# Two attention layers with routed experts: GpSimd's indirect DMAs moved to the end of a step, routing one step shorter, stores moved to SyncE

## The reference

```python
x = x + tanh(g_xattn[0]) * L0_xattn(layernorm(x), ctx, ctx)   # 16 heads of 8, softmax
x = x + tanh(g_ffn[0])   * L0_ffn(layernorm(x))               # 8 experts, top 2 per token, gelu
x = x + tanh(g_xattn[1]) * L1_xattn(ctx, ctx, layernorm(x))   # 16 heads of 8, masked softmax
x = x + tanh(g_ffn[1])   * L1_ffn(layernorm(x))               # 4 experts, all computed, weights gated
```

## Time and profile before

| | |
|---|---|
| three timed runs | 1296.69, 1297.87, 1298.11 us; median 1297.87 |
| the profiled execution's own time | 1297.54 us |
| its span, first to last instruction | 1295.9 us |
| busy share of the span | PE 89%, PEld 74%, DVE 72%, ACT 55%, POOL 47% |
| chain that ended last | PE 74%, issue 8%, POOL 5%, ACT 4%, DVE 4%, SPq 3%, DMA 1% |
| layer 0 attention, 20 to 335 us | PE busy 296.5 of 315.0, granted clock 0.97 |
| its tail and the plan, 335 to 419 us | PE busy 42.0 of 84.0, granted clock 0.68 |
| expert stage, 419 to 683 us | PE busy 258.4 of 264.0, POOL 153.3 |
| start of layer 1, 683 to 713 us | PE busy 5.7 of 30.0 |
| layer 1 attention, 713 to 1066 us | PE busy 328.3 of 353.0, granted clock 0.98 |
| dense experts, 1066 to 1296 us | PE busy 209.1 of 230.0 |

### The profile page before, as it was taken

The page is one execution under the profiler, slowest core; times in us unless marked ns, Lnnn a source line. Parts: engine busy times, 40 slices in busy tenths (PEclk is TensorE's granted clock), DMA queues, the critical chain, the costliest instruction groups (busy, mean ns, idle before and its releaser), DMA issues.

```text
span 1295.9 us, 41850 instructions
## 1 busy us (share of the span) xinstructions
PE 1147.0 (89%) x13375; PEld 965.1 (74%) x13375; DVE 933.0 (72%) x3267; ACT 718.8 (55%) x1554; POOL 613.2 (47%) x828
## 2 busy tenths in 40 slices
PE   4799999899861999999992899999899985999998
PEld 3577777677650999999991677777677765999997
DVE  4578888688756544444442799999898858888887
ACT  3588877688640555555550566666566642444443
POOL 2123555465675555665556555555555323121220
PEclk9899999899875999999995899999999997999999
DMA  6501111111112222222213222222222100000000
GB/s 187 183 27 35 53 58 52 44 51 53 49 40 79 74 73 73 73 73 73 69 58 108 67 68 67 66 66 65 60 71 61 50 2 1 25 17 24 16 24 25
DMA packets 85622, 76.42 MB, mean 59 GB/s; under 512 B 35160, under 2 KB 66648, under 8 KB 85464
## 3 DMA queue, kind: packets, MB, share of 16 engines
q1 hardware_dynamic: 73816, 48.14, 13.2%
q0 software_dynamic: 11648, 26.24, 6.5%
HBM read 50.21 MB, written 23.07 MB: 57 GB/s over the span
## 4 chain that ended last, share of the span: by engine, by line
PE 74%; issue 8%; POOL 5%; ACT 4%; DVE 4%; SPq 3%; DMA 1%; POOLq 1%; DVEq 0%; ACTq 0%
PE ps_m L1429 10%; PE ps_p L1636 9%; PE ps_m L1584 8%; PE ps_p L1417 8%; PE ps_s L1389 5%; PE ps_s L1379 5%; PE ps_s L1451 3%; PE ps_s L1570 3%; PE ps_s L1469 3%; PE ps_s L1624 2%; PE ps_s L1626 2%; PE ps_s L1572 2%; PE ps_s L1571 2%; PE ps_s L1625 2%; PE ps_m L1405 2%
## 5 line engine op out<-in xcount | busy, mean ns | idle before, releaser
L926 DVE TENSOR_REDUCE mx<-ps_s 128x8 f32<-128x512 f32 x256 | 169.9, 685 | 57.0 <-PE ps_s L1379 56.9
L1429 PEld LDWEIGHTS ps_m<-Vbd,PT 128*64 128x64 f32 x4096 | 140.2, 138 | 57.6 <-issue 52.3
L687 ACT ACTIVATE PT<-ps_p 128x512 f32<-128x512 f32 x256 | 153.0, 598 | 30.3 <-PE ps_p L1417 27.8
L1417 PE MATMUL ps_p<-cst,Pr 128*128 128x128 f32 x1024 | 161.8, 283 | 8.6 <-ACT PT L687 4.8
L1429 PE MATMUL ps_m<-Vbd,PT 128*64 128x18 f32 x4096 | 163.7, 213 | 0.1
L533 POOL TENSOR_TENSOR spare<-spare 1x1 f32<-1x1 f32 x148 | 29.2, 197 | 263.9 <-PE ps_s L1626 142.3
L844 ACT ACTIVATE Kbd<-ps_s,c 128x512 f32<-128x512 f32 x128 | 87.6, 687 | 118.1 <-PE ps_s L1626 117.6
L588 POOL DMA_INDIRECT w1a<-louts,gi x128 | 124.6, 973 | 41.1 <-issue 36.2
L1584 PE MATMUL ps_m<-xn3T 128*128 128x128 f32 x1152 | 140.0, 275 | 0.2 <-ACT xn3T L810 0.2
L1417 PEld LDWEIGHTS ps_p<-cst,Pr 128*128 128x128 f32 x1024 | 119.9, 145 | 22.8 <-issue 15.9
L1584 PEld LDWEIGHTS ps_m<-xn3T 128*128 128x128 f32 x1152 | 134.7, 192 | 0.4 <-issue 0.4
(11 more groups left out here) (209 smaller groups left out, 2659.7 us busy)
## 6 DMA issues: line engine op xcount, KB each, us to landing
ctxg<-in_ctxT SPq DMA_DIRECT2D x64, 256.0 KB, 2.7
xn3T<-lists SPq DMA_DIRECT2D x72, 128.0 KB, 2.1
louts<-xn3T POOLq DMA_DIRECT2D x72, 128.0 KB, 2.4
Kbd<-in_ctxT SPq DMA_DIRECT2D x512, 8.0 KB
out<-x SPq DMA_DIRECT2D x16, 256.0 KB, 2.3
w1a<-in_L_ffn_W SPq DMA_DIRECT2D x1, 2048.0 KB, 9.7
w1a<-louts,gi POOLq DMA_INDIRECT x128
lists<-xn3T,pos POOLq DMA_INDIRECT x96, 2.2
```

What stands on the lines that cost most here:

```text
L687: return nc.scalar.activation(dst, src, ACT.Copy)
L926: V.tensor_reduce(mx[g.par][:, q, :], per_key(ps_s[:, q, :]), AX, ALU.max).then_inc(max_done, 1)
L1417: ins = turn(ps_p[:, c % 2, P * i:P * i + P], Pr[g.par][:, j // 2, col:col + P], ident)
L1429: ins = mm((bank7, bank6)[pr][S * b:S * b + S, VW * j:VW * (j + 1)], PT[c][:, P * i + S * b:P * i + S * b + S], Vbd[g.par][:, 2 * pr + b, ...
```

## The change

- GpSimd's order in a step becomes: constant rows of g-1, inverse deviations, then the indirect DMAs. The wait for the scores is gone. In layer 0 the scattered group is g-8 rather than g-9.
- `both_choices` joins `second_choice` inside step e+4, `ranks` moves to the end of step e+4, `route_places` to the start of step e+5.
- Tail blocks are routed in steps 28, 30, 32 and 34 rather than 29, 31, 33 and 34; the scatters of the last steps are dealt out in slots, six indirect DMAs in each of the steps 28 to 32, ten in step 33, none in 34, eight in 35.
- The stores of the expert stage go from GpSimd to SyncE, where they stand between the loads: load of tile k+6, store of tile k.

```diff
--- before.py
+++ after.py
@@ -84,8 +84,9 @@
 
 MAIN = GROUPS - STEPS
 RB = 4
-TAIL = {25: 29, 27: 31, 29: 33, 31: 34}
-LAST_ROWS = {29: (20,), 30: (21, 22), 31: (23, 24), 32: (25, 26), 33: (27,), 34: (28, 29), 35: (30, 31)}
+TAIL = {25: 28, 27: 30, 29: 32, 31: 34}
+LAST_ROWS = {28: ((20, 0, 1), (21, 0)), 29: ((21, 1), (22, 0, 1)), 30: ((23, 0, 1), (24, 0)), 31: ((24, 1), (25, 0, 1)),
+             32: ((26, 0, 1), (27, 0)), 33: ((27, 1), (28, 0, 1), (29, 0, 1)), 34: (), 35: ((30, 0, 1), (31, 0, 1))}
 BLOCKS = MAIN // RB + len(TAIL)
 
 
@@ -501,11 +502,22 @@
                 sp.dma_start(xin[k % 4], lists[bass.ds(r, ET), :].rearrange("(t p) d -> p t d", p=P)).then_inc(
                     rows_in[k % 4], 16)
 
-            for k in range(4):
+            def store_rows(u, k):
+
+                sp.wait_ge(yo_ready, at(u, k, 1, 1, 4))
+                sp.dma_start(louts[sl(at(u, k, ET, 0, 4), ET), :].rearrange("(t p) d -> p t d", p=P),
+                             yo[k % 2]).then_inc(rows_out[k % 2], 16)
+
+            for k in range(8):
                 load_rows(0, k)
-            with sp.Fori(1, NT // 4) as u:
+                if k >= 6:
+                    store_rows(0, k - 6)
+            with sp.Fori(2, NT // 4) as u:
                 for k in range(4):
                     load_rows(u, k)
+                    store_rows(u, k - 6)
+            for k in range(NT - 6, NT):
+                store_rows(0, k)
             sp.wait_ge(yo_ready, NT)
 
             for dst, src in ((v1.rearrange("p (e f) -> p e f", e=E1), A["L1_ffn_ew1"].rearrange("e d f -> d e f")),
@@ -556,12 +568,12 @@
                                         orow[g.layer][:, :].unsqueeze(1).to_broadcast([P, 2, DM]),
                                         ALU.add).then_inc(xc_ready, 1)
 
-            def scatter(g):
+            def scatter(g, slots):
 
                 pool.wait_ge(pos_ready, g.block(1))
                 pool.wait_ge(xn2_ready, g.count(2, 2))
                 carry(lambda: touch(g.par), g.at())
-                for slot in range(2):
+                for slot in slots:
                     for t in range(2):
                         if g.in_main():
                             i = 2 * (g.k % RB) + t
@@ -589,42 +601,28 @@
                                                      bass.IndirectOffsetOnAxis(ap=gi[i][:, c:c + 1], axis=0)
                                                      ).then_inc(gathered[i], 16)
 
-            def apart_from_scores(g):
-
-                if g.real():
-                    pool.wait_ge(s_done, g.count(4, 4))
-
             def step(g):
                 def have(d):
                     return g.plus(d).real()
 
-                if g.layer == 0:
-                    if isinstance(g.u, int) and g.k in LAST_ROWS:
-                        for k in LAST_ROWS[g.k]:
-                            scatter(Group(0, k, 0))
-                    elif have(-9):
-                        apart_from_scores(g)
-                        scatter(g.plus(-9))
-                if g.layer == 1 and have(4):
-                    apart_from_scores(g)
-                    gather(g.plus(4))
-                if g.layer == 1 and have(-1):
+                if have(-1):
                     rows_plus_constant(g.plus(-1))
                 if have(-2) or have(2):
                     inverse_deviations(g)
-                if g.layer == 0 and have(-1):
-                    rows_plus_constant(g.plus(-1))
+                if g.layer == 0:
+                    if isinstance(g.u, int) and g.k in LAST_ROWS:
+                        for k, *slots in LAST_ROWS[g.k]:
+                            scatter(Group(0, k, 0), slots)
+                    elif have(-8):
+                        scatter(g.plus(-8), (0, 1))
+                elif have(4):
+                    gather(g.plus(4))
 
             nc.gpsimd.memset(mask_in, 0.0).then_inc(mask_clear, 1)
             pool.wait_ge(setup_in, SETUP)
             pool.wait_ge(x_in0, 16)
             pool.wait_ge(orow_done, 1)
             steps(pool, 0, step)
-
-            def store_rows(u, k):
-                pool.wait_ge(yo_ready, at(u, k, 1, 1, 4))
-                pool.dma_start(louts[sl(at(u, k, ET, 0, 4), ET), :].rearrange("(t p) d -> p t d", p=P),
-                               yo[k % 2]).then_inc(rows_out[k % 2], 16)
 
             def low_weights(u, k):
 
@@ -641,11 +639,8 @@
             with pool.Fori(0, NT // 4 - 1) as u:
                 for k in range(4):
                     low_weights(u, k + 2)
-                    store_rows(u, k)
-            for k in range(NT - 4, NT):
-                if k + 2 < NT:
-                    low_weights(0, k + 2)
-                store_rows(0, k)
+            for k in range(NT - 4, NT - 2):
+                low_weights(0, k + 2)
             pool.wait_ge(rows_out[0], 16 * (NT // 2))
             pool.wait_ge(rows_out[1], 16 * (NT // 2))
             pool.wait_ge(place_ready, 1)
@@ -1086,12 +1081,9 @@
                 if g.layer == 0:
                     if isinstance(g.u, int) and g.k == 3:
                         layer1_constants()
-                    block = router_due(g, -6, 1)
+                    block = router_due(g, -5, 1)
                     if block:
                         route_places(block)
-                    block = router_due(g, -5, None)
-                    if block:
-                        both_choices(block)
                     now(statistics_in, 2)
                     now(maximum, 0, 2)
                     now(maximum, 0, 3)
@@ -1109,6 +1101,7 @@
                     block = router_due(g, -4, None)
                     if block:
                         second_choice(block)
+                        both_choices(block)
                     now(heads, -1, 0)
                     now(denominators, -1, 1)
                     now(heads, -1, 1)
@@ -1359,7 +1352,7 @@
                 if g.plus(-4).real():
                     pe.wait_ge(lg_read, g.plus(-4).count(1, 1))
                 pe.wait_ge(kq_ready, g.count(1, 1))
-                ranks_before = router_due(g, -6, 1) if g.layer == 0 else None
+                ranks_before = router_due(g, -5, 1) if g.layer == 0 else None
                 if ranks_before:
                     pe.wait_ge(rank_read, ranks_before.block(1))
                 wait(pe, exp_done, g.count(4, -3))
@@ -1516,7 +1509,7 @@
                     now(probs_by_values, -1, 3)
                     now(logits, -3)
                     now(values, 1)
-                    block = router_due(g, -5, 0)
+                    block = router_due(g, -4, 0)
                     if block:
                         ranks(block, g)
                 else:
```

## The result

The changed kernel takes **1313.93 us** (median of four executions, 1313.15 to 1320.38), the kernel before 1297.99 in the same session (1296.69 to 1299.16). The ratio is **1.0135**, interval 1.0107 to 1.0164. By the medians the change costs 16 us, where the forecast was 1300.1 us with 1309 as its upper end.

The account below looks back on a forecast made before the run. The prediction took the chain of waits, mostly TensorE's, with GpSimd's 5% in three places, to bound the kernel. Its terms, 11.5 + 6.4 + 0 - 8.4 - 2.9 - 3.9 - 0.5 = +2.2, on 1297.87 gave 1300.1 us, range 1290 to 1309.

Parts of the forecast that it names:

- part 3: Layer 0, behind the new TensorE pauses: the granted clock falls, 1.6 us each, +6.4 us in all, bounds 0 and 8.4.
- slower: Whole kernel: a time more than 0.2% (2.6 us) above that of the kernel before; chance 0.50.
- Parts 1 and 2: Layer 0: GpSimd's scatters land late, so VectorE's write of `pos` waits and TensorE stalls at four steps, +11.5 us.
- Part 4: Layer 0, `both_choices` inside the step: about 0.8 us more operations, covered by slack, 0, bound +1.5 us over five blocks.
- Part 5: Tail of layer 0: long steps at 28 and 30, last scatter starts near 414 as before, 0, bounds -3 and +3 us.
- Part 6: Expert stage: without stores ahead, GpSimd starts the rest of the weights earlier, -8.4 us, bounds -11 and -4.
- Part 7: Last store of the expert stage: on SyncE ahead of the weight loads it takes 2.2 us, not 5.12: -2.9 us.
- Part 8: Layer 1: deviations no longer stand behind a gather, -3.9 us at its start and -0.5 us at step 24.
- the clock holds: Rival, layer 0: stalls come but TensorE's pauses don't cost the clock; 1293.7 us without the 6.4; chance 0.13.
- GpSimd and VectorE block each other: Rival, layer 0: indirect DMAs wait for VectorE's normalisations, landing 1.2 us later per stall, +4.8 us, 1305 us; chance 0.06.

Follow-up runs that it names:

- two buffers against one: The changed kernel with two buffers for the integer places `pos`, so its write no longer waits for the scatters of the block before: 1285.36 us, ratio 0.9885.
- the kernel with these parts alone: The kernel before with stores on SyncE and, in layer 1 only, constant rows and deviations ahead of the gather: 1283.02 us, ratio 0.9876.

## Why the prediction was wrong

**The step that failed is part 3, the clock.** It took 1.6 us per stall, 6.4 in all, with 2.1 each as the upper bound. By the medians it cost 18, 4.3 to 6.0 per stall in the profiles. The bound came from one step with a pause, in the tail, where the clock had been back soon; that was taken for the worst case, though the new pauses stand at another place of the step, with other work behind them. With 18 in the place of 6.4 the sum is 2.2 + 11.6 = 13.8, or 1311.7, and 1313.93 was measured. The error was in the bound as much as in the value: with 2.1 per stall the sum could not reach the result. The runs show what stood in its place: behind a stall the clock stays at 0.50 for about twice as long as behind the pause that was read, and what TensorE works on there decides it in part; why a given pause costs the clock at all stays open. By direction the prediction had given "slower" the highest chance, 0.50, but its own number lay within 0.2% of no change.

The other steps:

- *Parts 1 and 2*, the order and the wait: right in place, cause and size. Four pauses of 2.71, 2.92, 2.94 and 2.79 us, 11.4 in all against 11.5; step 20 spared. The kernel with the order alone adds that the shorter routing is not needed for the stall. Parts 2 and 3 together were put at 17.9 and cost 28.6 (two buffers against one).
- *Part 4*: 0 was right. Step 7 took 0.4 more, step 8 0.2 less.
- *Part 5*, the tail: 0, bounds 3. The last scatter starts 34.3 us later than before, where stalls and clock had added 30.0 ahead of step 28 and 7.1 in it, so the tail's own share is -2.8, inside the bounds. It is partly luck: the wait of 4.97 us that the new tail removes was not in the reckoning. Against the old tail it is nothing to 2 us better with GpSimd's new order; with the old order routing and tail together cost 6 us. The long steps came at 28 and 30 as forecast, and a part of their length is the clock again.
- *Part 6*: -8.4, measured -9.7. The wait for the rest of the weights went as forecast; most tiles stand 3.43 apart instead of 3.45 to 3.5, and one in four 3.6.
- *Part 7*: -2.9, measured -3.2. The stores landed in 1.8 us at the median from SyncE and in 2.4 from GpSimd, 0.6 apart. The rest went with the place ahead of the weight loads: in the kernel before 5.12 us was the last store's alone, and no other took more than 2.8. That the queue of loads is the cause was argued and not tested by itself. The Trainium skill ("DMA: Bandwidth & Descriptors", section "Latency and other measured facts") gives a first byte after about 0.6 us for a DMA with hardware descriptors, as SyncE's are, and about 1 us for one with software descriptors, as GpSimd's are. The trace agrees with the direction of these 0.4 us, and going by the row was right for the whole.
- *Part 8*: -3.9 and -0.5. The pause of TensorE fell by 7.35, of which the stores alone give 3.6 and the order in layer 1, added to them, 3.65. Step 24 is 1.16 shorter and step 25 0.76 longer: -0.4. Parts 6 to 8 were put at -15.7 together, and the kernel with these parts alone measured -15.7 (1283.0 against 1298.7); that the sum meets so exactly is luck, as single terms are off by up to 1.5.

Of the rivals, "the clock holds" was the wrong direction to look in: the doubt about the clock was given only to the cheap side. That GpSimd and VectorE block each other changed nothing in the time: the write of `pos` came at +13.17 where +13.03 was reckoned without it. But that they don't disturb each other at all, as the prediction read from one case, goes too far. The second of a step's four scatters, which now often stands beside line 875, landed 2.67 us after its issue at the median where it took 2.23 before; the last two of the four were as quick as before, and on the last one the write waits.

The Trainium skill ("TensorE: Matmul & The Clock Gate", section "HAM oscillation — how this bites in real kernels") tells of a kernel whose waits for a DMA, of about 3 to 5 us, cost the clock anew each time. The trace agrees that it is paid each time, and with shorter pauses: four of four of 2.7 to 2.9 us did, with 4.3 to 6.0 us each.

## What to carry to other kernels

Before work is moved to the end of an engine's step, look for who reuses its inputs: a single small buffer, written a little later by another engine, can wait for the very last of the moved DMAs, and doubling it cost 64 bytes a partition here. Price a new pause of TensorE with what runs behind it, not only by its own length: here 2.9 us of pause cost up to 6.0 more. Twelve useless matmuls of 512 columns, which filled the pause, saved it; seven saved a part and three nothing. Time the parts of a change alone: here two of them were worth 15.7 us (1283.0 against 1298.7), and a third, the order in layer 0 with one buffer, gave away more than that.

## What had not been expected of the hardware

- The granted clock fell behind pauses of 1.3 to 2.2 us and held behind others of 1.07 and 1.48, at the same place of the step.
- After the stalls of steps 16 and 24 the clock stayed at 0.50 through more than 13 us of unbroken work of TensorE. With 12 matmuls of 512 columns among this work it was back after less than 7. Which property of the work decides was not separated.
- The fall can come late: at step 16 with 7 matmuls, 2.4 us after TensorE was busy again.
- At the turn of layer 1's loop the pause was 2.46 us in the profile of before, and the clock held. In the profile after it was 2.91 and the clock fell, and the two steps around it took 3.0 us more:

```profile
945.58 0.18 PE L1481 MATMUL ps_p<-ones 128*128 128x1 bf16 x1 [2.91 <-issue]
```

  In each other profile but the one of before (leaving out the chip with the granted clock of 0.84) it fell too, behind pauses from 2.42 up, also in the kernel with the stores alone, whose layer 1 is that of before. The two steps took 25.5 to 27.1 us there, against 24.1. So this is no cost of the change, and the row on which the bound 0 for the clock rested was an exception.
